# Rotary attention: the causal mask moved from TensorE products to a GpSimd select on the exponentials, with TensorE two score groups ahead

## The reference, cut to what matters

```python
x = x + _L1_attn_b_ref(_layernorm(x, axis=-1), wq, wk, wv, wo)

def _L1_attn_b_ref(x, wq, wk, wv, wo):     # 16 heads of 8 features
    Q, K, V = (split_heads(x @ w.T) for w in (wq, wk, wv))
    Q, K = _rope(Q, 10000.0), _rope(K, 10000.0)
    scores = jnp.einsum('bhqd,bhkd->bhqk', Q, K) / math.sqrt(8)
    causal_mask = jnp.triu(jnp.ones((256, 256), dtype=bool), k=1)
    scores = jnp.where(causal_mask, -jnp.inf, scores)
    attn = jax.nn.softmax(scores, axis=-1)
    out = jnp.einsum('bhqk,bhkd->bhqd', attn, V)
    return out.transpose(0, 2, 1, 3).reshape(2, 256, 128) @ wo.T
```

## Time and profile before

| | us |
|---|---|
| median of 3 runs | 2896.11 (2887.38 to 2908.32) |
| the profiled execution | 2902.76 |
| its span | 2900.9 |
| mean granted TensorE clock | 0.723 of full speed |

### The profile page before, as it was taken

How to read it: one execution, slowest core, us unless ns; L and a number is a source line. 1 busy time by engine, 2 the same in 40 slices (tenths; PEclk the granted TensorE clock), 3 DMA queues, 4 the chain that set the end, 5 groups by cost and what they waited for, 6 DMA issues and landing times.

```text
span 2900.9 us, 44112 instructions
## 1 busy us (share of the span) xinstructions
PE 1753.3 (60%) x13716; PEld 1146.8 (40%) x13716; DVE 1334.2 (46%) x3558; ACT 970.8 (33%) x1719; POOL 1057.4 (36%) x1177
## 2 busy tenths in 40 slices
PE   3765506776666454556776676422325488888975
PEld 2544404555444242244554454100124234455443
DVE  3648811222334677473222333543215466666644
ACT  3651102232223321312232222356761123444342
POOL 2001777724651774757714651771000200000000
PEclk9985557778878655557788787655555568998985
DMA  8941118999997111117999997120000000000001
GB/s 234 382 181 29 51 53 275 325 304 292 321 289 241 52 52 54 52 55 244 327 308 294 310 301 241 51 54 8 4 2 0 0 1 1 1 1 2 1 1 29
DMA packets 332506, 393.39 MB, mean 136 GB/s; under 512 B 57952, under 2 KB 222512, under 8 KB 332208
## 3 DMA queue, kind: packets, MB, share of 16 engines
q1 hardware_dynamic: 215616, 171.43, 19.0%
q10 hardware_dynamic: 83984, 153.13, 15.4%
q0 software_dynamic: 32768, 67.17, 7.7%
HBM read 242.13 MB, written 164.63 MB: 140 GB/s over the span
## 4 chain that ended last, share of the span: by engine, by line
PE 36%; DVE 15%; DMA 13%; ACT 11%; issue 10%; SPq 9%; POOL 6%; DVEq 0%; ACTq 0%; POOLq 0%
DMA arena<-expert_blocks 12%; SPq L1819 6%; ACT arena L955 5%; PE psum L1918 4%; PE psum L1909 4%; POOL slot_rows L1725 4%; PE psum L448 3%; SPq L1815 3%; PE psum L1347 2%; PE psum L1900 2%; PE psum L1328 2%; PE psum L432 2%; PE psum L993 1%; PE psum L427 1%; ACT arena L1210 1%
## 5 line engine op out<-in xcount | busy, mean ns | idle before, releaser
L1736 POOL DMA_INDIRECT arena<-slot_results,SLOTS x512 | 490.7, 958 | 503.1 <-DMA slot_results<-arena 285.8
L1725 POOL DMA_INDIRECT slot_rows<-arena,SLOTS x512 | 493.4, 964 | 309.4 <-issue 308.8
L1699 DVE COPY arena<-psum 128x512 f32<-128x512 f32 x288 | 198.6, 690 | 742.3 <-PE psum L1918 719.4
L1909 PE MATMUL psum<-arena 128*64 128x128 f32 x2304 | 236.5, 336 | 278.4 <-DMA arena<-expert_blocks 271.0
L1779 ACT ACTIVATE arena<-psum 128x512 f32<-128x512 f32 x288 | 171.9, 597 | 476.4 <-PE psum L1900 467.6
L1909 PEld LDWEIGHTS psum<-arena 128*64 128x64 f32 x2304 | 154.5, 165 | 349.0 <-issue 291.5
L169 POOL TENSOR_SCALAR rstd<-mv 128x4 f32<-128x4 f32 x32 | 6.2, 193 | 772.3 <-DVE mv L577 771.8
L1900 PE MATMUL psum<-ident,arena 128*128 128x128 f32 x1152 | 231.6, 335 | 84.9 <-DMA arena<-slot_rows 84.3
L1918 PE MATMUL psum<-arena 64*128 64x128 f32 x2304 | 253.3, 350 | 0.0
L1786 ACT ACTIVATE arena<-psum 128x256 f32<-128x256 f32 x288 | 110.4, 383 | 338.5 <-PE psum L1909 335.3
L1918 PEld LDWEIGHTS psum<-arena 64*128 64x128 f32 x2304 | 189.6, 230 | 64.4 <-issue 64.2
(11 more groups left out here) (234 smaller groups left out, 3064.5 us busy)
## 6 DMA issues: line engine op xcount, KB each, us to landing
arena<-expert_blocks SPq DMA_DIRECT2D x1152, 96.0 KB
arena<-slot_rows ACTq DMA_DIRECT2D x288, 256.0 KB
slot_results<-arena ACTq DMA_DIRECT2D x288, 256.0 KB
slot_rows<-zeros SPq DMA_DIRECT2D x2, 18432.0 KB, 84.2
slot_rows<-arena,SLOTS POOLq DMA_INDIRECT x512, 2.2
arena<-slot_results,SLOTS POOLq DMA_INDIRECT x512
expert_blocks<-in_expert_w SPq DMA_DIRECT2D x1, 7680.0 KB, 26.0
expert_blocks<-in_expert_w SPq DMA_DIRECT2D x1, 5120.0 KB, 52.7
```

The lines of the kernel that those rows point to most:

```text
L1699: dve.tensor_copy(YSB[:, p].rearrange("p (c h) d -> p h c d", h=2), psum[:, first:first + 2, 0:256].rearrange("p h (c d) -> p h c d", c=2) ...
L1725: pool.indirect_dma_start(out=slot_rows[h], out_offset=bass.IndirectOffsetOnAxis(ap=SLOTS[:, t, k:k + 1], axis=0), in_=XNH[:, t], in_offse ...
L1736: pool.indirect_dma_start(out=GATHERED[:, t % TPI, k], out_offset=None, in_=slot_results[h], in_offset=bass.IndirectOffsetOnAxis(ap=SLOTS[ ...
L1909: mm = pe.matmul(psum[lo:lo + INTER, 2 + 5 * (p % 2), o:o + P], EWB[:, p, q, 0:INTER], XSBT[:, p, P * q:P * q + P], start=True, stop=True, ...
```

## The change

Five edits, all of them in the rotary layer:

1. `mask_scores` is no longer called there. `diagonal_first` replaces `head_scores`. It makes the same two products per head, but lays the three blocks of 128 queries so that the two diagonal blocks stand beside each other.
2. The exponential writes `PR2` in the order block, head, query. `PR2` holds four groups in place of two.
3. POOL gets `causal(i)`: for each group, as soon as `r_exp` allows, one `affine_select` in place over the 1024 elements per partition of the eight diagonal blocks. It sets to zero what has the key later than the query, and then raises `r_sel`. `values` on PE waits for `r_sel` in place of `r_exp`.
4. PE issues the scores of groups 0 and 1 ahead of everything, and inside the loop those of group g+2 ahead of the values of group g (before: g+1). The 32 probe heads are moved along: heads 0 to 3 now stand between the scores of group 1, 4 to 7 between those of group 2.
5. ACT runs its other work one exponential later, so as to match.

```diff
--- before.py
+++ after.py
@@ -427,6 +427,12 @@
             pe.matmul(psum[:, bank, 0:256], kt[0:k, 0:128], qt[0:k, :], start=True, stop=False, skip_group_check=True)
             pe.matmul(psum[:, bank, 256:384], kt[0:k, 128:256], qt[0:k, 128:256], start=False, stop=False, skip_group_check=True)
 
+        def diagonal_first(pe, bank, kt, qt, k):
+
+            v = psum[:, bank, 0:384].rearrange("p (b q) -> p b q", q=P)
+            pe.matmul(v[:, 0:3:2, :], kt[0:k, 0:128], qt[0:k, :].rearrange("k (b q) -> k b q", q=P), start=True, stop=True, skip_group_check=True)
+            return pe.matmul(v[:, 1, :], kt[0:k, 128:256], qt[0:k, 128:256], start=True, stop=True, skip_group_check=True)
+
         def mask_scores(pe, bank):
             v = psum[:, bank, :].rearrange("p (a q) -> p a q", q=256)[:, :, 0:128]
             return pe.matmul(v, identb[:], mask_kq[:].unsqueeze(1).broadcast_to([P, 2, P]), start=False, stop=True, skip_group_check=True)
@@ -447,7 +453,7 @@
                         lo, hi = (0, 256) if kt == 0 else (128, 256)
                         mm = pe.matmul(psum[32 * r:32 * r + 32, 3, 256 * half + lo:256 * half + hi],
                                        ones4[:, head_of(n, r) % 4, :] if half else vp(kt, head_of(n, r)),
-                                       pr[:, r, 0:256] if kt == 0 else pr[:, r, 256:384],
+                                       pr(kt, r),
                                        start=(n == half == kt == 0), stop=(n == 3 and half == kt == 1),
                                        skip_group_check=True, tile_position=(0, 32 * r))
             return mm
@@ -497,7 +503,8 @@
                 if n == 0:
                     pe.wait_ge(a_vp.sem, a_vp.at(0, i))
                     pe.wait_ge(a_ot.sem, a_ot.before(0, i))
-                weigh_values(pe, n, lambda kt, h: VP[:, u, 2 * (h // 8) + kt, h % 8, :], PR[:, n % 2]).then_inc(a_av.sem, 1)
+                weigh_values(pe, n, lambda kt, h: VP[:, u, 2 * (h // 8) + kt, h % 8, :],
+                             lambda kt, r: PR[:, n % 2, r, 256 * kt:384 if kt else 256]).then_inc(a_av.sem, 1)
 
             def output(i):
                 pe.wait_ge(a_ot.sem, a_ot.at(0, i))
@@ -1034,7 +1041,8 @@
         QT2 = view([P, 2, 2, NH // 2, SEQ], BF16)
         KT2 = view([P, 2, 2, NH // 2, SEQ], BF16)
         VP2 = view([P, 2, TPI, NH, 32])
-        PR2 = view([P, 2, 4, 384])
+        PARTS = 4
+        PR2 = view([P, PARTS, 3, 4, P])
         REC2 = view([P, SEQ])
         OT2 = view([P, 2, SEQ])
         MX = view([P, TPI, NH])
@@ -1055,6 +1063,7 @@
         r_mrows = signal("r_mrows", 5)
         r_sc = signal("r_sc", 8, start=START + 8)
         r_exp = signal("r_exp", 8, start=START + 8)
+        r_sel = signal("r_sel", 8)
         r_av = signal("r_av", 8, start=START + 8)
         r_rec = signal("r_rec", 2)
         r_ot = signal("r_ot", 2)
@@ -1206,30 +1215,30 @@
 
             def weigh(i, g):
                 act.wait_ge(r_sc.sem, r_sc.at(0, i, g + 1))
-                act.wait_ge(r_av.sem, r_av.at(0, i, g - 1))
-                act.activation(PR2[:, g % 2], psum[:, 4:8, 0:384], ACT.Exp, scale=DH ** -0.5).then_inc(r_exp.sem, 1)
+                act.wait_ge(r_av.sem, r_av.at(0, i, g - PARTS + 1))
+                act.activation(PR2[:, g % PARTS].rearrange("p b r q -> p r b q"), psum[:, 4:8, 0:384].rearrange("p r (b q) -> p r b q", q=P), ACT.Exp, scale=DH ** -0.5).then_inc(r_exp.sem, 1)
 
             def step(i, u, left=STEPS):
                 weigh(i, 0)
                 weigh(i, 1)
+                weigh(i, 2)
                 if left >= 2:
                     tokens(i + 2)
-                weigh(i, 2)
+                weigh(i, 3)
                 if left >= 2:
                     projected(i + 2, 0)
-                weigh(i, 3)
+                weigh(i, 4)
                 if left >= 2:
                     projected(i + 2, 1)
-                weigh(i, 4)
+                weigh(i, 5)
                 if left >= 2:
                     projected(i + 2, 2)
                     projected(i + 2, 3)
-                weigh(i, 5)
                 weigh(i, 6)
+                weigh(i, 7)
                 if left >= 1:
                     transposed(i + 1, 1 - u, 8)
                     transposed(i + 1, 1 - u, 9)
-                weigh(i, 7)
                 if left >= 1:
                     transposed(i + 1, 1 - u, 10)
                     transposed(i + 1, 1 - u, 11)
@@ -1279,6 +1288,15 @@
                     pool.tensor_copy(VP2[:, u, :, n:NH:4, DH * n:DH * n + DH],
                                      QKV3[:, 2].rearrange("p t (h d) -> p t h d", d=DH)[:, :, n:NH:4, :]).then_inc(r_vp.sem, 1)
 
+            def causal(i):
+
+                for g in range(8):
+                    pool.wait_ge(r_exp.sem, r_exp.at(0, i, g + 1))
+                    stand(pool)
+                    diagonal = PR2[:, g % PARTS, 0:2].rearrange("p b r q -> p (b r) q")
+                    pool.affine_select(diagonal, diagonal, [[0, 8], [1, P]], ALU.is_ge, 0.0, base=0,
+                                       channel_multiplier=-1).then_inc(r_sel.sem, 1)
+
             norm(0)
             values(0, 0)
             norm(1)
@@ -1286,11 +1304,16 @@
             norm(2)
             with pool.Fori(0, STEPS // 2 - 2) as i2:
                 for u in range(2):
+                    causal(i2 * 2 + u)
                     norm(i2 * 2 + u + 3)
                     values(i2 * 2 + u + 2, u)
+            causal(STEPS - 4)
             norm(STEPS - 1)
             values(STEPS - 2, 0)
+            causal(STEPS - 3)
             values(STEPS - 1, 1)
+            causal(STEPS - 2)
+            causal(STEPS - 1)
 
         def rope_tensor(pe, layer):
             r = front_run(layer)
@@ -1353,21 +1376,21 @@
                     pe.wait_ge(r_kt.sem, r_kt.at(0, i))
                 pe.wait_ge(r_exp.sem, r_exp.at(0, i, g))
                 for rr in range(4):
-                    head_scores(pe, 4 + rr, head(KT2, u, b, head_of(n, rr)), head(QT2, u, b, head_of(n, rr)), SCORE_K)
+                    mm = diagonal_first(pe, 4 + rr, head(KT2, u, b, head_of(n, rr)), head(QT2, u, b, head_of(n, rr)), SCORE_K)
+                    if rr == 3:
+                        mm.then_inc(r_sc.sem, 1)
                     if between is not None:
                         between()
-                for rr in range(4):
-                    mm = mask_scores(pe, 4 + rr)
-                mm.then_inc(r_sc.sem, 1)
 
             def values(i, u, g, between=None):
                 b, n = g // 4, g % 4
-                pe.wait_ge(r_exp.sem, r_exp.at(0, i, g + 1))
+                pe.wait_ge(r_sel.sem, r_sel.at(0, i, g + 1))
                 if g == 0:
                     pe.wait_ge(r_vp.sem, r_vp.at(0, i))
                 if n == 0:
                     pe.wait_ge(r_ot.sem, r_ot.at(0, i, b))
-                weigh_values(pe, n, lambda kt, h: VP2[:, u, 2 * b + kt, h, :], PR2[:, g % 2], between).then_inc(r_av.sem, 1)
+                weigh_values(pe, n, lambda kt, h: VP2[:, u, 2 * b + kt, h, :],
+                             lambda kt, r: PR2[:, g % PARTS, 1, r, :] if kt else PR2[:, g % PARTS, 0:3:2, r, :], between).then_inc(r_av.sem, 1)
 
             def output(i):
                 pe.wait_ge(r_ot.sem, r_ot.at(0, i))
@@ -1387,10 +1410,12 @@
                     pe.wait_ge(r_qt.sem, r_qt.at(0, i + 1, 3))
                     pe.wait_ge(r_kt.sem, r_kt.at(0, i + 1, 3))
                 scores(i, u, 0)
+                some = one if left >= 1 else None
+                scores(i, u, 1, some)
                 for g in range(8):
                     between = one if g < 4 and left >= 1 else None
-                    if g < 7:
-                        scores(i, u, g + 1, between)
+                    if g < 6:
+                        scores(i, u, g + 2, some if g < 3 else None)
                     if g == 0 and not first:
                         output(i - 1)
                     if g == 1 and left >= 2:
```

## The result

The changed kernel takes 2921.84 us (median of 12 runs, 2909.86 to 2926.95) against 2894.93 us for the kernel before beside it (12 runs). The ratio is 1.0087, 95% interval 1.0072 to 1.0102. That is 27 us lost, where the forecast was no measurable change. It is less than the 1% bound, but the interval excludes no change.

The account below looks back on a forecast made before the run. No engine was over 60% busy; PE bounds a rotary step's middle, a DVE chain its second half. Full steps -10.2 and ends -4.2 make -14.4 us, selects add +13.2: -1.2 on 2896.1, about 2895, range 2876 to 2930.

Parts of the forecast that it names:

- -1.7 + 2.2: Full rotary step: 1.7 us gained by masks leaving PE, against two selects in DVE's turn costing 1.1 us each.
- my lower bound: Length of one select on POOL, from its copies: at least 1.13 us for 1024 elements; upper bound 2.5, taken 1.8.
- rival 2: Turn: each select holds DVE for its whole length, 21.6 us in place of 13.2, giving 2903 us; chance 0.17.
- The ends: Steps 6 and 7: masks leaving give 2.6 and 3.5 us, waits for a select cost about 1.9; together -4.2.
- The first select of a step: Start of a step: group 0's select ends before its values come after 2566, so its latency is hidden.
- the middle: Step's part up to 2592.23: PE hardly idle, three masks leave (-1.35 us), group 5's scores come in (+0.45).
- Rival 4: Start of a step: the new wait prolongs PE's lower clock, 1.7 us per step, +10 in six, 2905; chance 0.08.
- rival 1: Turn: selects don't hold DVE up, the whole -14.4 us is kept, 2882, or 2870 without the new wait; chance 0.22.

Follow-up runs that it names:

- no_select: The changed kernel without the selects, so nothing masks the rotary layer's scores and values wait for the exponential; ratio to the kernel before 1.0065.
- hybrid_ballast: hybrid_fill with two dummy products of 512 columns ahead of the scores of groups 2, 3 and 4; ratio to the kernel before 0.9959.
- all_selects_ballast: hybrid_ballast with all eight groups' selects on POOL again and the first not held back; ratio to the kernel before 1.0015.
- turn_free: The changed kernel with groups 5, 6 and 7 masked on TensorE and the first select held until the normalisation is done; ratio to the kernel before 1.0079.
- after_fill: The changed kernel with dummy products at the start of a step: 6 after group 0's scores, 3 after group 1's, 8 ahead of probe head 2; ratio 0.9998.
- before_fill: The kernel before with dummy products at the start of a step: 6 after group 0's scores, 8 ahead of probe head 2; ratio 0.9970.
- before_no_masks: The kernel before without its 256 mask products in the rotary layer and nothing in their place; ratio to the kernel before 1.0137.
- output_early: The changed kernel with the previous step's output product moved between the scores of groups 1 and 2; ratio to the kernel before 1.0132.
- after_ballast: The changed kernel with two dummy products of 512 columns ahead of the scores of every group; ratio to the kernel before 1.0108.
- order_only: The changed kernel's order and layout, with all masks as TensorE products again and no select; ratio to the kernel before 1.0062.
- hybrid_fill: The changed kernel with start-of-step dummy products, early output product, selects only for groups 0 to 4 (first held back), TensorE masks for 5 to 7; ratio 0.9981.

## Why the prediction was wrong

**Right.** The masks left PE (13460 products in place of 13716). ACT's `rows` starts at the end of the turn. The selects of groups 6 and 7 fall into the turn and hold DVE. PE waits for the exponential of group 1 (0.89 us, 1.2 forecast). Step 7 needs 2813.75 - 2811.69 = 2.06 us per group in five of its seven intervals (2.15 forecast). For an ordinary full step my terms gave -1.7 + 2.2 = +0.5 us, and step 4 has 58.4 against 58.0. That match is in part luck: with no select at all the step is 55.5, so what is taken off is worth 2.5 and not 1.7, and the selects cost 2.9 and not 2.2.

**Sizes that were off and met by chance.** The select was taken at 1.8 us and takes 1.09, just under my lower bound of 1.13 from the copies. In return it holds DVE for 0.89 us, that is 82% of its length; I had scaled two thirds from copies too short to show it. Both are slowed in turn: the select of 2675.36 comes while DVE's L1092 has 0.56 us left and takes 1.50 in place of 1.09, and the first DVE operation behind L1092 takes 1.31 us in place of 0.42 and ends only after the select. The Trainium skill ("SBUF — State Buffer", "Who interferes with whom") calls the shared pair of ports an exclusive lock and lets the order of issue decide who blocks; these numbers agree with it. With the right length, rival 2 would have been 12 x 1.09 = 13 us. The ends were also off: step 6 gives nothing (45.5 against 45.3 us) and step 7 gives 1.4 us, so together -1.2 in place of -4.2.

**A term that was missing.** "The first select of a step stands behind the deviations and the copies of POOL ... so that is hidden as well." I asked only whether PE waits for it. The select runs at 2639.13, straight after those copies, and there it meets the normalisation, for which in turn the probe heads wait. L597 takes 1.99 us in place of 1.22 (0.77 us more), and all probe heads of the step come later. In all, the selects cost 2.9 us in an ordinary full step (no_select against the changed kernel) to 3.4 (hybrid_ballast against all_selects_ballast, 19 us in the time), not 2.2.

**The step that failed.** It is the middle: "What is taken off PE here is gained". I priced the four masks of a group at 0.45 us, the full-clock price, and took for granted that the rest of PE's work keeps its price when they go. Rival 4 had the right mechanism, but at 1.7 us per step, only "over the four probe heads and scores behind" the new wait, and with a chance of 0.08. What happened is larger: some steps don't come back to full clock at all until their second half, and then the whole middle is done at the lower level, which costs 10 to 17 us per step. In the profiled execution that is +5.9 us in step 0 and +15.0 in step 3, 21 of the 24.7 us. In step 3 PE is busy 12.7 us longer than before with 32 products fewer. So where the sum had 0.4 us gained up to the end of the middle, one step lost 15 us. The kernel before already had a long step, its step 0 with 0.76 granted and 63.6 us [shown above]. My rows took step 3 as the pattern and left that one out, and it could have been the warning.

**Smaller slips in the working.** The 12 us that rival 1 adds for a start without the new wait are worked out nowhere (six waits of 1.2 us are 7). And "about 1%" as what a measurement can tell was far too wide: with 12 runs of each kernel the interval is 0.3% wide.

How much is clock and how much hold? With the hold and the clock helped (all_selects_ballast) the difference to before is +5.5 us; without the hold and with nothing for the clock (turn_free) it is +26. They are not a sum, since both contain the savings and the new order, and since dummy work is in one. But the whole loss is there without the hold, it is gone with the hold where dummy products keep the level up (after_fill), and no version that does nothing for the clock was faster than before. The Trainium skill ("TensorE: Matmul & The Clock Gate", Part 1) has the low level as the default that activity releases; before_fill and before_no_masks agree with it in both directions. Its sentence that the ramp penalty is "<1% of a typical kernel span" does not cover this kernel, where leaving out the masks cost 1.37%.

**Not settled.** What decides which steps fall. Steps with the same work ran at 58 and at 73 us within one execution, output_early made it worse although it closed a gap, and after_ballast evened the steps out without gaining. Nor is it settled how much of the changed kernel's loss comes from the missing masks and how much from the new order: each alone lost 23 us or more (order_only, before_no_masks), both together 26 (no_select), so they don't add up. Each profile is one execution, so the positions of the long steps are examples. The medians over 6 to 12 runs carry the verdicts. The 23 us of order_only are seen in part: its new wait is 1.54 to 1.62 us, and its granted clock is 0.83 to 0.86 in most full steps where before has 0.91. The price of the hold was not measured with the order of before.

## What to carry to other kernels

Before taking products off TensorE, look at its granted clock step by step, the worst step included; where it already falls in some, price the rest of its work at both levels, and try a few dummy products in its waits first, which is a cheap test (here -0.3% alone). Closing a single gap is no such test: output_early did that and lost 48 us. Before giving work to GpSimd, list what VectorE does at that moment from SBUF to SBUF (here a rotation with two SBUF inputs and a normalisation), on its critical stretches above all, also where nobody waits for the GpSimd result; then move the select away from them or leave those groups on TensorE.

## What the runs showed of the hardware that was not expected

- Leaving out 256 mask products (an estimate of 29 us of PE at full clock, 64 x 0.45 from the earlier trace rows) and changing nothing else made the kernel 52 us slower (1.0137), and adding up to 14 dummy products at the start of each step made it 13 us faster (0.9970).
- A busy PE stayed at the lower level: in step 3 of the changed kernel the granted clock was 0.50 for 51.2 us on end (2564.4 to 2615.6), with PE busy 48.2 of them.
- A step of the same instructions took 51.7 us at a granted clock of 1.00 and 66.8 at 0.72, next to each other in one execution (hybrid_fill).
- A GpSimd `affine_select` on 1024 fp32 elements per partition takes 1.09 us, no more than the 1.13 estimated for a copy, and beside VectorE operations with two SBUF inputs 1.42 to 1.50. Each one that met the turn held VectorE for 0.89 us.
